# A two-block sandwich kernel: another order of its prologue, and constant matmuls where TensorE would wait in it

## The chip, the cores and the metric

The kernel runs on one core of one Trainium2 chip. The metric is the device time of one execution in microseconds (us), the median of several runs. Engines are named as in the profile: PE is TensorE's matmul, PEld its weight load, DVE is VectorE, ACT is ScalarE, POOL is GpSimd, SP is SyncE, which here only issues DMAs.

## What is computed

Cut to what matters, with x of 16 x 1024 rows of D = 256, E = 8 experts, C = 320 rows each, H = 1024:

```python
def block1(x):                       # x: (16, 1024, 256)
    g = sigmoid(x @ Wg.T + bg)
    h_t = (1 - g_t) * h_(t-1) + g_t * x_t        # along the 1024 rows of a sequence
    return h @ Wo.T + bo

def block2(xf):                      # xf: (16384, 256)
    eid = argmax(softmax(xf @ router_w + router_b))
    rank = number of earlier rows with the same eid
    valid = rank < C
    y_tok = relu(row @ w1[eid] + b1[eid]) @ w2[eid] + b2[eid]     # where valid
    yov = relu(xf @ ow1 + ob1) @ ow2 + ob2                        # elsewhere
    return y_tok where valid, else yov

x = x + layernorm(block1(layernorm(x)))
x = x + layernorm(block2(layernorm(x)))
```

## The kernel before

The 16384 rows are worked in 32 groups of 512 (`GT`), two groups to a sequence, written as pairs (i, v): sequence i, half v. The helper `grp` steps through them. Every fp32 product is made of three matmuls on a high and a low part: `split_product` (L1067 on) multiplies high by high, high by low and low by high; the high part is made by ACT (a copy into the fp32r type), the low part by DVE or POOL (a subtraction). So each operand `X` stands as `X_hi` and `X_lo`.

A group goes through: statistics of its rows (DVE, `stats0`, L712 to L724), 1/sqrt of the variance and the scaled mean (POOL, `deviation`, L372 and L374), the normalised rows `tok` (POOL, `norm0`, L383), their transposes into PSUM tile `psT` (PE, `transposes0`, L1084), `xnT_hi` and `xnT_lo` (L578, L745), the gate product into `psA` (PE, `gate`), the sigmoid `keep` (ACT, L584), the recurrence as a scan (DVE, `recurrence`: `ngx` L755, `hst` L761), `hst_hi` (ACT, L592) and `hst_lo` (POOL, `state_lo`, L424), the product with Wo (PE, `project`), `att` (DVE, `attended`, L767), statistics again (`stats1`), normalisation (ACT, `norm1`, L562), the residual into `x1` (DVE, L780), statistics (`stats2`), `tok2` (POOL, `norm2`, L415), transposes (PE, `transposes1`, L1127), `xfT_hi` and `xfT_lo` (L599, L802), and then the router (`route`), the overflow network on all rows (`layer1`, `layer2`, hidden rows L552, L556, L858) and a scatter of the rows to the experts' buffer `xbuf` in DRAM (POOL). After the 32 groups eight expert steps work on the buffers.

In the loop these are software-pipelined: `step(i, u)` on PE runs the overflow network of group now, `project` of the next and `gate` of the one after it. **The prologue** is what must run before step 0: the whole chain above for group (0,0), up to `xfT_lo`, and the first half, up to the scan, for group (0,1). In it also stand the transposing of Wg and Wo, and the split of the overflow weights ow1 and ow2: four pieces of 128 x 1024, made high by ACT (L662) and low by DVE (L983), out of `stage`, into `W1[1]` and `W2[1]`. Step 0 works a group whose first two tiles cannot overflow (`sure`), so its products have 256 rows and not 512.

Each engine has an order of its own, written by hand in its block function, and semaphores between them; an engine works its instructions strictly in that order. SP's order is x (0,0), Wg, Wo, three bias loads, x (0,1), three broadcasts, router_w, ow1, ow2, b2 and then the clearing of `xbuf` (2.6 MB). ow1 and ow2 share one semaphore, so ACT waits for both.

PSUM tile `psY` (two banks) is written by `layer2` alone and so not used before step 0.

Of the kernel before, what the change touches and what calls it, by code (L numbers as in the profile page):

```python
# [55 lines left out]
def sandwich_kernel(nc, x, Wg, bg, Wo, bo, router_w, router_b, w1, b1, w2, b2, ow1, ob1, ow2, ob2, out):  # L56
# [6 lines left out]
    with ExitStack() as ctx:  # L63
# [474 lines left out]
        def _(act):  # L538
# [118 lines left out]
            xn_hi((0, 1))  # L657
            act.wait_ge(s_w["ow"], 32)
            for m, W in enumerate((W1, W2)):
                for q in range(2):  # L660
                    dst = W[1][0][:].rearrange("p a b -> p (a b)")
                    act.activation(dst[:, q * 1024:(q + 1) * 1024], stage[:, m, q * 1024:(q + 1) * 1024], ACT.Copy)\  # L662
                        .then_inc(s_ow_hi, 1)
# [41 lines left out]
        def _(dve):  # L705
# [271 lines left out]
            def overflow_lo(m):  # L977
                W = (W1, W2)[m]
                for q in range(2):
                    hi = W[1][0][:].rearrange("p a b -> p (a b)")[:, q * 1024:(q + 1) * 1024]  # L980
                    dst = W[1][1][:].rearrange("p a b -> p (a b)")[:, q * 1024:(q + 1) * 1024]
                    dve.wait_ge(s_ow_hi, 2 * m + q + 1)
                    dve.tensor_tensor(dst, stage[:, m, q * 1024:(q + 1) * 1024], hi.bitcast(F32), ALU.subtract)\  # L983
                        .then_inc(s_ow_lo, 1)

            stats0((0, 0))
            for n, W in enumerate((WgT, WoT)):
# [296 lines left out]
```

## Time and profile before

| | before |
|---|---|
| median of 3 runs | 1213.2 us (1212.72 to 1214.56) |
| the profiled execution, its own time | 1212.57 us |
| its span in the trace | 1210.8 us |
| PE busy | 1149.2 us (95%), 7657 matmuls |
| DVE busy | 1015.6 us (84%) |
| ACT busy | 733.8 us (61%) |
| POOL busy | 711.8 us (59%) |
| mean granted TensorE clock | 0.984 |

Times in the trace count from the start of the span. A row of a timeline gives start, duration, engine, line and operation; a count at its end (x4) means that the row merges so many, and its duration is that of them all. Matmuls overlap, so their pace is read from one start to the next. The granted clock is 1.0 at 2.4 GHz and 0.5 at 1.2 GHz.

### The profile page before, as it was taken

To read this page: it belongs to the slowest core of one execution; us is meant where nothing else is said; L and a number is where in the kernel's file an instruction comes from. 1 tells how busy PE (TensorE), PEld (TensorE's weight loads), DVE (VectorE), ACT (ScalarE), POOL (GpSimd) and SP (SyncE) were. 2 spreads that over 40 slices of the span, in tenths; PEclk is the share of its full clock that TensorE was granted. 3 is DMA by queue.
4 is the path that set the end of the run, shared out by engine and by line. 5 is a ranking of instruction groups with operands and counts; after the bars stand their busy time and mean duration, and the time that the engine had idled before them with its cause. 6 is when DMAs were issued, how large, how long until landed. Compare 5 with 4: busy or idle time off the path is not lost.

```text
span 1210.8 us, 24630 instructions
## 1 busy us (share of the span) xinstructions
PE 1149.2 (95%) x7657; PEld 1027.6 (85%) x7657; DVE 1015.6 (84%) x2792; ACT 733.8 (61%) x1293; POOL 711.8 (59%) x826
## 2 busy tenths in 40 slices
PE   5489999999999999999999999999999999899995
PEld 4378888888888888888888888888888888898985
DVE  4688888889888898889888888888889878688883
ACT  3256666666566566666666665556656666678773
POOL 4565666656665656565656666656656664345564
PEclk8799999999999999999999999999999999999997
DMA  8211111111111111111100110011111100445421
GB/s 253 87 36 44 53 50 47 42 37 35 35 35 35 35 35 35 35 35 35 35 28 25 35 35 28 24 35 35 35 35 35 35 18 18 121 136 159 169 81 33
DMA packets 59430, 65.05 MB, mean 54 GB/s; under 512 B 7835, under 2 KB 55629, under 8 KB 59268
## 3 DMA queue, kind: packets, MB, share of 16 engines
q1 hardware_dynamic: 52228, 59.32, 15.3%
q0 software_dynamic: 7168, 5.32, 1.5%
q8 instruction: 16, 0.26, 0.1%
q14 instruction: 18, 0.15, 0.0%
HBM read 40.17 MB, written 38.61 MB: 65 GB/s over the span
## 4 chain that ended last, share of the span: by engine, by line
PE 84%; DVE 6%; POOL 3%; ACT 3%; issue 3%; DMA 0%; DVEq 0%; ACTq 0%; POOLq 0%
PE psY L1171 11%; PE psY L1174 10%; PE psY L1173 10%; PE psH L1071 10%; PE psH L1073 10%; PE psH L1072 10%; PE psA L1071 5%; PE psA L1073 5%; PE psA L1072 5%; PE psT L1127 3%; PE psT L1084 2%; DVE st L712 2%; POOL rstd L372 1%; PE psT L1133 1%; PE psT L1135 1%
## 5 line engine op out<-in xcount | busy, mean ns | idle before, releaser
L372 POOL TENSOR_TENSOR rstd<-veps,mhalf 128x4 f32<-128x4 f32 (+1 forms) x144 | 195.9, 1361 | 386.0 <-DVE nmean L724 386.0
L552 ACT ACTIVATE hid<-psH,biasT 128x512 f32<-128x512 f32 (+2 forms) x320 | 206.7, 646 | 268.8 <-PE psH L1073 264.5
L1171 PE MATMUL psY<-W_hi,hid_hi 128*128 128x256 f32 x1200 | 346.1, 288 | 3.4 <-DVE hid_lo L858 3.4
L1174 PE MATMUL psY<-W_hi,hid_lo 128*128 128x256 f32 x1200 | 339.1, 283 | 0.0
L1173 PE MATMUL psY<-W_lo,hid_hi 128*128 128x256 f32 x1200 | 338.8, 282 | 0.0
L1071 PE MATMUL psH<-xfT_hi,W_hi 128*128 128x512 f32 (+2 forms) x640 | 240.9, 376 | 1.6 <-DVE xfT_lo L802 1.6
L1073 PE MATMUL psH<-xfT_hi,W_lo 128*128 128x512 f32 (+2 forms) x640 | 239.6, 374 | 0.0
L1072 PE MATMUL psH<-xfT_lo,W_hi 128*128 128x512 f32 (+2 forms) x640 | 239.1, 374 | 0.0
L858 DVE TENSOR_TENSOR hid_lo<-hid,hid_hi 128x512 fp32r<-128x512 f32 (+2 forms) x320 | 203.4, 649 | 40.9 <-ACT hid_hi L556 32.1
L1171 PEld LDWEIGHTS psY<-W_hi,hid_hi 128*128 128x128 f32 x1200 | 226.6, 189 | 12.8 <-DVE hid_lo L858 3.1
L1173 PEld LDWEIGHTS psY<-W_lo,hid_hi 128*128 128x128 f32 x1200 | 226.9, 189 | 6.6
L1174 PEld LDWEIGHTS psY<-W_hi,hid_lo 128*128 128x128 f32 x1200 | 226.4, 189 | 0.0
L556 ACT ACTIVATE hid_hi<-hid 128x512 fp32r<-128x512 f32 (+2 forms) x320 | 190.5, 595 | 10.2
L393 POOL DMA_INDIRECT xbuf<-x,idx x128 | 150.4, 1175 | 37.8 <-issue 35.1
L1073 PEld LDWEIGHTS psH<-xfT_hi,W_lo 128*128 128x128 f32 x640 | 120.6, 188 | 21.9
L1071 PEld LDWEIGHTS psH<-xfT_hi,W_hi 128*128 128x128 f32 x640 | 121.0, 189 | 19.5 <-issue 2.4
L1072 PEld LDWEIGHTS psH<-xfT_lo,W_hi 128*128 128x128 f32 x640 | 121.0, 189 | 14.0
L415 POOL TENSOR_SCALAR tok<-x,rstd,nmr 128x256 f32<-128x256 f32 x124 | 109.2, 892 | 8.5 <-POOL nmr L374 8.5
L570 ACT ACTIVATE ysb<-ysb,nmr,rstd 128x256 f32<-128x256 f32 x147 | 76.7, 591 | 45.2 <-POOL nmr L374 44.7
L424 POOL TENSOR_TENSOR hst_lo<-hst,hst_hi 128x512 fp32r<-128x512 f32 x64 | 82.4, 1316 | 10.5 <-ACT hst_hi L592 8.9
L584 ACT ACTIVATE keep<-psA,neg_bg 128x512 f32<-128x512 f32 x64 | 44.0, 689 | 69.0 <-PE psA L1073 69.0
L1071 PE MATMUL psA<-WoT_hi,hst_hi 128*128 128x256 f32 x256 | 75.9, 297 | 2.0 <-POOL hst_lo L424 2.0
(113 smaller groups left out, 2069.2 us busy)
## 6 DMA issues: line engine op xcount, KB each, us to landing
xin<-L_attn_x SPq DMA_DIRECT2D x32, 512.0 KB, 3.5
stage<-L_ffn_w SPq DMA_DIRECT2D x16, 1024.0 KB, 5.6
out<-outt SPq DMA_DIRECT2D x31, 512.0 KB, 2.9
xbuf<-zrow SPq DMA_DIRECT2D x1, 2570.0 KB, 18.7
xin<-xbuf SPq DMA_DIRECT2D x8, 257.0 KB, 5.6
stage<-L_ffn_ow SPq DMA_DIRECT2D x2, 1024.0 KB, 10.1
xbuf<-x,idx POOLq DMA_INDIRECT x128
b_b<-L_ffn_b SPq DMA_DIRECT2D x1, 1024.0 KB, 13.3
```

What stands on the lines that cost most here:

```text
L372: pool.tensor_tensor(rstd[k][:, t0:n], veps[k][:, t0:n], mhalf[:, t0:n], ALU.pow).then_inc(s_rs[k], 1)
L393: pool.indirect_dma_start(out=xbuf, out_offset=bass.IndirectOffsetOnAxis(idx[v][:, t:t + 1], 0), in_=x1[v][:, t, 0:ROW], in_offset=None, b ...
L415: last = pool.tensor_scalar(tok2[:, t, :], x1[v][:, t, 0:D], rstd[2][:, t:t + 1], nmr[2][:, t:t + 1], ALU.mult, ALU.add)
L552: act.activation(hid[j % 2][:, at:n], psH[:, j % 2, at:n], ACT.Relu, bias=bias).then_inc(s_hid, 1)
L556: act.activation(hid_hi[j % 4][:, at:n], hid[j % 2][:, at:n], ACT.Copy).then_inc(s_hid_hi, 1)
L858: dve.tensor_tensor(hid_lo[j % 4][:, at:n], hid[j % 2][:, at:n], hid_hi[j % 4][:, at:n].bitcast(F32), ALU.subtract).then_inc(s_hid_lo, 1)
L1071: pe.matmul(dst, w_hi, r_hi, start=(k == 0), stop=False)
L1072: pe.matmul(dst, w_hi, r_lo, start=False, stop=False)
L1073: return pe.matmul(dst, w_lo, r_hi, start=False, stop=(k == last_k))
L1171: pe.matmul(psY_t[:, t, :], hi, w[0][:, j, :], start=(j == 0 and t % 2 == 0), stop=False, skip_group_check=True)
L1173: pe.matmul(psY_t[:, t, :], hi, w[1][:, j, :], start=False, stop=False, skip_group_check=True)
L1174: last = pe.matmul(psY_t[:, t, :], lo_, w[0][:, j, :], start=False, stop=(j == HC - 1), skip_group_check=True)
```

## The change

It changes nothing in the loop and the experts' part but two waits of step 0. In the prologue:

- SP: ow2 and ow1 are loaded right behind x (0,1), ahead of the broadcasts and router_w, each with a semaphore of its own; SP then waits for both before it issues b2 and the clearing of `xbuf`.
- DVE: makes `tok` of group (0,0), the normalised `att`, `tok2` (by `norm2`, a function that the experts' part already had) and `hst_lo` of both groups, which POOL and ACT made before. The four W_lo pieces stand singly between other work; the statistics of (0,1) come behind `xnT_lo`; the recurrence of (0,1) is cut in two, with `xfT_lo` between the halves.
- ACT: the four W_hi pieces stand singly, the two of ow2 around the first group's sigmoid and `hst_hi`.
- POOL: keeps the four deviations and `tok` of (0,1).
- PE: group (0,0) is transposed a second time into `psA` and not into `psT`, so it need no longer wait for `ngx` of (0,1); that wait and the one for rw_lo stand ahead of `route` in step 0.
- PE: `keep_clock(n)` multiplies `ones` (128 x 128, bf16) by itself, repeated to 512 columns, into `psY`, n times, with nothing that reads it: 5, 3, 5, 12, 3, 24 and 6 times, 58 in all, at the places below.

```diff
             load((0, 1))
+            sp.dma_start(stage_w2(), ow2.rearrange("(c p) d -> p c d", p=P)).then_inc(s_w["ow2"], 16)
+            sp.dma_start(stage_w1(), ow1.rearrange("(c p) h -> p c h", p=P)).then_inc(s_w["ow1"], 16)
...
-            sp.dma_start(stage_w1(), ow1.rearrange("(c p) h -> p c h", p=P)).then_inc(s_w["ow"], 16)
-            sp.dma_start(stage_w2(), ow2.rearrange("(c p) d -> p c d", p=P)).then_inc(s_w["ow"], 16)
+            sp.wait_ge(s_w["ow2"], 16)
+            sp.wait_ge(s_w["ow1"], 16)
...
-            norm0((0, 0))
-            pool.wait_ge(s_tok, 1)
+            deviation(0, (0, 0), TG)
             norm0((0, 1))
-            state_lo((0, 0))
             deviation(1, (0, 0), TG)
-            norm2((0, 0))
-            state_lo((0, 1))
+            deviation(2, (0, 0), TG)
...
             xn_hi((0, 0))
+            overflow_hi(1, 0)
             act.wait_ge(s_biasT, 2)
             sigmoid((0, 0))
-            state_hi((0, 0))
+            state_hi((0, 0), (0,))
+            overflow_hi(1, 1)
+            state_hi((0, 0), (1,))
+            xn_hi((0, 1))
             act.wait_ge(s_w["rw"], 16)
             act.activation(rw[:, :, 0:E], rw_raw[:], ACT.Copy).then_inc(s_rw_hi, 1)
...
-            norm1((0, 0))
+            overflow_hi(0, 0)
+            overflow_hi(0, 1)
             sigmoid((0, 1))
-            xf_hi((0, 0), GT)
+            xf_hi((0, 0), GT, turned=psA)
             state_hi((0, 1))
...
+            def first_rows(k, dst, src):
+                dve.wait_ge(s_nm[k], 1)
+                for t in range(TG):
+                    last = dve.tensor_scalar(dst[:, t, :], src[:, t, 0:D], rstd[k][:, t:t + 1], nmr[k][:, t:t + 1],
+                                             ALU.mult, ALU.add)
+                return last
...
+            stats0((0, 0))
+            turned_lo(0, WgT)
+            first_rows(0, tok, xin[0]).then_inc(s_tok, 1)
+            turned_lo(1, WoT)
             dve.wait_ge(s_biasT, 1)
             dve.tensor_scalar(neg_bg[:], biasT[:, BG:BG + DC], -1.0, None, ALU.mult).then_inc(s_biasT, 1)
+            xn_lo((0, 0))
             stats0((0, 1))
-            xn_lo((0, 0))
+            overflow_lo(1, 0)
             recurrence((0, 0))
-            dve.wait_ge(s_rw_hi, 1)
-            dve.tensor_tensor(rw[:, :, E:2 * E], rw_raw[:], rw[:, :, 0:E].bitcast(F32), ALU.subtract).then_inc(s_rw_lo, 1)
+            state_lo((0, 0))
             xn_lo((0, 1))
+            overflow_lo(1, 1)
             dve.wait_ge(s_w["bcast"], 48)
             attended((0, 0))
             stats1((0, 0))
-            overflow_lo(0)
+            overflow_lo(0, 0)
+            dve.wait_ge(s_att, 2)
+            first_rows(1, att, att).then_inc(s_u, 1)
             residual1((0, 0))
             stats2((0, 0))
-            recurrence((0, 1))
-            overflow_lo(1)
-            xf_lo((0, 0), GT)
+            overflow_lo(0, 1)
+            dve.wait_ge(s_x1, 1)
+            norm2((0, 0), x1, TG)
+            recurrence((0, 1), (0,))
+            xf_lo((0, 0), GT, turned=psA)
+            recurrence((0, 1), (1,))
+            dve.wait_ge(s_rw_hi, 1)
+            dve.tensor_tensor(rw[:, :, E:2 * E], rw_raw[:], rw[:, :, 0:E].bitcast(F32), ALU.subtract).then_inc(s_rw_lo, 1)
+            state_lo((0, 1))
             stats0((1, 0))
...
+            def keep_clock(n):
+                for _ in range(n):
+                    pe.matmul(psY[:, 0, :], ones[:], ones[:].unsqueeze(1).to_broadcast([P, TG, P]), start=True, stop=True)
+
             pe.wait_ge(s_const, 1)
+            keep_clock(5)
...
                     layer1(now, 0, GT, W1[1], at=sure(now) * P)
+                    if not live(grp(i, u, -1), NG):
+                        pe.wait_ge(s_rw_lo, 1)
+                        pe.wait_ge(s_ngx, cnt(nxt, 2, 2))
                     route(now)
...
+            keep_clock(3)
             transposes0((0, 0))
+            keep_clock(5)
             pe.wait_ge(s_wT_lo, 2)
             gate((0, 0))
+            keep_clock(12)
             pe.wait_ge(s_ngx, cnt((0, 0), 2, 2))
             transposes0((0, 1))
+            keep_clock(3)
             project((0, 0))
             gate((0, 1))
-            transposes1((0, 0), TG)
-            pe.wait_ge(s_rw_lo, 1)
+            keep_clock(24)
+            pe.wait_ge(s_tok2, 1)
+            pe.wait_ge(s_keep, cnt((0, 1), 2, 2))
+            for c in range(DC):
+                for t in range(TG):
+                    last = pe.transpose(psA[:, c, t * P:(t + 1) * P], tok2[:, t, c * P:(c + 1) * P], ident[:])
+                last.then_inc(s_T1, 1)
+            keep_clock(6)
             pe.wait_ge(s_ow_lo, 4)
```

On DVE, behind the statistics of `att` of group (0,0), before (`mv`, `veps`, `nmean` are steps of the statistics, `x_0` is `x1`):

```order
L983 TENSOR_TENSOR W_lo<-stage,W_hi 128x1024 [waits s_ow_hi] x2
L780 TENSOR_TENSOR x_0<-att,xin 128x4x256 [waits s_u]
L712 BN_STATS st<-x_0 128x6 [waits s_x1]
L712 BN_STATS st<-x_0 128x6 x3
L719 BN_AGGR mv<-st 128x2 [waits s_st2]
L719 BN_AGGR mv<-st 128x2 x3
L723 TENSOR_SCALAR veps<-mv 128x4 [waits s_ag2,s_nm2]
L724 TENSOR_SCALAR nmean<-mv 128x4
L755 SCALAR_TENSOR_TENSOR ngx<-keep,psT 128x512 [waits s_keep]
```

and in the changed kernel (its `tok` is the tile `tok2`):

```order
L986 TENSOR_TENSOR W_lo<-stage,W_hi 128x1024 [waits s_ow_hi]
L996 TENSOR_SCALAR att<-att,rstd,nmr 128x256 [waits s_nm1,s_att]
L996 TENSOR_SCALAR att<-att,rstd,nmr 128x256 x3
L783 TENSOR_TENSOR x_0<-att,xin 128x4x256 [waits s_u]
L715 BN_STATS st<-x_0 128x6 [waits s_x1]
L715 BN_STATS st<-x_0 128x6 x3
L722 BN_AGGR mv<-st 128x2 [waits s_st2]
L722 BN_AGGR mv<-st 128x2 x3
L726 TENSOR_SCALAR veps<-mv 128x4 [waits s_ag2,s_nm2]
L727 TENSOR_SCALAR nmean<-mv 128x4
L986 TENSOR_TENSOR W_lo<-stage,W_hi 128x1024 [waits s_ow_hi]
L900 TENSOR_SCALAR tok<-x_0,rstd,nmr 128x256 [waits s_T1,s_nm2,s_x1]
```

Both normalisations now stand in DVE's own queue, each behind one W_lo piece, and the scan of (0,1) behind the second of them.

On DVE, the first group's recurrence and what follows it, before:

```order
L755 SCALAR_TENSOR_TENSOR ngx<-keep,psT 128x512 [waits s_keep]
L761 SCALAR_TENSOR_TENSOR hst<-keep,ngx 128x512 [waits s_ngx]
L997 TENSOR_TENSOR rw<-rw_raw,rw 128x2x8 [waits s_rw_hi]
L745 TENSOR_TENSOR xnT_lo<-psT,xnT_hi 128x512 [waits s_xn_hi,s_gate]
L745 TENSOR_TENSOR xnT_lo<-psT,xnT_hi 128x512 [waits s_xn_hi]
L767 TENSOR_TENSOR att<-psA,bo_b 128x512 [waits s_wo,s_w_bcast]
```

and in the changed kernel:

```order
L758 SCALAR_TENSOR_TENSOR ngx<-keep,psT 128x512 [waits s_keep]
L764 SCALAR_TENSOR_TENSOR hst<-keep,ngx 128x512 [waits s_ngx]
L1007 TENSOR_TENSOR hst_lo<-hst,hst_hi 128x512 [waits s_h_hi,s_scan] x2
L748 TENSOR_TENSOR xnT_lo<-psT,xnT_hi 128x512 [waits s_xn_hi,s_gate]
L748 TENSOR_TENSOR xnT_lo<-psT,xnT_hi 128x512 [waits s_xn_hi]
L986 TENSOR_TENSOR W_lo<-stage,W_hi 128x1024 [waits s_ow_hi]
L770 TENSOR_TENSOR att<-psA,bo_b 128x512 [waits s_wo,s_w_bcast]
```

`hst_lo` came to this queue from POOL, and a W_lo piece stands ahead of `att`.

On PE, from the end of the first group's gate to its product with Wo, before (only the first row of each kind of the last product):

```order
L1073 MATMUL psA<-xnT_hi,WgT_lo 128x512
L1084 MATMUL psT<-ident,tok 128x128 [waits s_tok,s_ngx]
L1084 MATMUL psT<-ident,tok 128x128 x7
L1071 MATMUL psA<-WoT_hi,hst_hi 128x256 [waits s_h_lo,s_h_hi,s_keep]
L1072 MATMUL psA<-WoT_lo,hst_hi 128x256
```

and in the changed kernel:

```order
L1110 MATMUL psA<-xnT_hi,WgT_lo 128x512
L1090 MATMUL psY<-ones 128x512 x12
L1121 MATMUL psT<-ident,tok 128x128 [waits s_tok,s_ngx]
L1121 MATMUL psT<-ident,tok 128x128 x7
L1090 MATMUL psY<-ones 128x512 x3
L1108 MATMUL psA<-WoT_hi,hst_hi 128x256 [waits s_h_lo,s_h_hi,s_keep]
L1109 MATMUL psA<-WoT_lo,hst_hi 128x256
```

The constant matmuls have no wait of their own: twelve stand ahead of the transposes of (0,1), three between them and the product.

## Rows read from the trace of the kernel before

**Rows 1.** The page: busy time of PE, and its granted clock in 40 slices

```profile
PE 1149.2 (95%) x7657; PEld 1027.6 (85%) x7657; DVE 1015.6 (84%) x2792; ACT 733.8 (61%) x1293; POOL 711.8 (59%) x826
PEclk8799999999999999999999999999999999999997
```

**Rows 2.** Stretches: length, busy us of PE, PEld, DVE, ACT, POOL; granted clock, DMA, GB/s

```profile
18.30:20.20 1.90, 0.16 (x1) 0.00 (x0) 1.86 (x3) 1.17 (x2) 0.00 (x0) 1.00 1.02 358
23.90:27.20 3.30, 3.29 (x15) 3.30 (x16) 0.49 (x2) 3.08 (x4) 0.00 (x0) 0.50 1.05 251
35.00:47.00 12.00, 0.00 (x0) 0.00 (x0) 9.24 (x17) 2.18 (x5) 7.01 (x6) 0.61 0.16 46
49.06:59.30 10.24, 8.62 (x54) 7.34 (x54) 7.04 (x23) 4.12 (x9) 6.06 (x8) 0.72 0.41 146
50.70:54.60 3.90, 3.82 (x14) 2.80 (x15) 2.54 (x11) 1.49 (x4) 3.49 (x4) 0.50 0.65 218
76.00:80.00 4.00, 4.00 (x19) 3.47 (x18) 3.16 (x11) 1.48 (x4) 3.23 (x4) 0.67 0.28 99
193.00:500.00 307.00, 307.00 (x2026) 272.18 (x2025) 267.83 (x750) 187.43 (x318) 193.25 (x227) 1.00 0.11 34
```

**Rows 3.** Timeline, POOL, in the prologue

```profile
8.23 2.18 POOL L383 TENSOR_SCALAR tok<-xin,rstd,nmr 128x256 f32<-128x256 f32 x4 [0.25 <-POOL nmr L374]
20.50 3.26 POOL L424 TENSOR_TENSOR hst_lo<-hst,hst_hi 128x512 fp32r<-128x512 f32 x2 [5.60 <-ACT hst_hi L592]
31.69 1.91 POOL L372 TENSOR_TENSOR rstd<-veps,mhalf 128x4 f32<-128x4 f32 x1 [7.92 <-DVE nmean L724]
39.67 1.01 POOL L372 TENSOR_TENSOR rstd<-veps,mhalf 128x4 f32<-128x4 f32 x1 [5.75 <-DVE nmean L724]
41.81 5.33 POOL L415 TENSOR_SCALAR tok<-x,rstd,nmr 128x256 f32<-128x256 f32 x4 [0.24 <-POOL nmr L374]
50.47 2.51 POOL L424 TENSOR_TENSOR hst_lo<-hst,hst_hi 128x512 fp32r<-128x512 f32 x2 [3.33 <-ACT hst_hi L592]
```

**Rows 4.** Timeline, DVE and ACT, from the first group's recurrence to step 0

```profile
18.40 1.22 DVE L761 TENSOR_TENSOR_SCAN hst<-keep,ngx 128x512 f32<-128x512 f32 x1
28.60 0.69 DVE L767 TENSOR_TENSOR att<-psA,bo_b 128x512 f32<-128x512 f32 x1 [0.99 <-PE psA L1073]
29.32 1.40 DVE L712 BATCH_NORM_STATS2 st<-att 128x6 f32<-128x256 f32 x4
31.52 2.35 DVE L983 TENSOR_TENSOR W_lo<-stage,W_hi 128x1024 fp32r<-128x1024 f32 x2
33.96 2.07 ACT L562 ACTIVATE att<-att,nmr,rstd 128x256 f32<-128x256 f32 x4 [6.98 <-POOL nmr L374]
36.07 1.23 DVE L780 TENSOR_TENSOR x<-att,xin 128x1024 f32<-128x1024 f32 x1 [2.20 <-ACT att L562]
58.02 1.28 DVE L767 TENSOR_TENSOR att<-psA,bo_b 128x512 f32<-128x512 f32 x2
```

**Rows 5.** Timeline, DVE in the experts' part: four rows normalised by DVE

```profile
1016.68 1.38 DVE L897 TENSOR_SCALAR tok<-x,rstd,nmr 128x256 f32<-128x256 f32 x4 [0.21 <-POOL nmr L374]
```

**Rows 6.** Timeline, PE: transposes and products at either clock

```profile
16.21 0.63 PE L1073 MATMUL psA<-xnT_hi,WgT_lo 128*128 128x512 f32 x1
16.64 0.63 PE L1071 MATMUL psA<-xnT_hi,WgT_hi 128*128 128x512 f32 x1
31.15 0.40 PE L1072 MATMUL psA<-xnT_lo,WgT_hi 128*128 128x512 f32 x1
31.38 0.39 PE L1073 MATMUL psA<-xnT_hi,WgT_lo 128*128 128x512 f32 x1
47.20 1.97 PE L1127 MATMUL psT<-ident,tok 128*128 128x128 f32 x8 [14.72 <-POOL tok L415]
60.41 1.03 PE L1084 MATMUL psT<-ident,tok 128*128 128x128 f32 x8
```

**Rows 7.** DMA issues at 6.72 us: KB each, us from issue to landing

```profile
stage<-L_ffn_ow SPq DMA_DIRECT2D x1, 1024.0 KB, 11.3
```

More of the change, by code:

```diff
@@ L164, in sandwich_kernel @@
         s_xbuf0 = sem("s_xbuf0")
-        s_w = {n: sem(f"s_w_{n}") for n in ("wg", "wo", "rw", "ow", "bias", "bcast", "b2")}
+        s_w = {n: sem(f"s_w_{n}") for n in ("wg", "wo", "rw", "ow1", "ow2", "bias", "bcast", "b2")}
         s_const = sem("s_const")
@@ L585, in sigmoid, with state_hi, xf_hi @@
                         .then_inc(s_keep, 1)
-            def state_hi(g):
+            def state_hi(g, cs=range(DC)):
                 i, v = g
                 act.wait_ge(s_wo, cnt(g, 2, 0))
-                for c in range(DC):
+                for c in cs:
                     act.wait_ge(s_scan, cnt(g, 2, c + 1))
                     act.activation(hst_hi[:, c, :], hst[v][:, c, :], ACT.Copy).then_inc(s_h_hi, 1)
-            def xf_hi(g, n, base=0):
+            def xf_hi(g, n, base=0, turned=psT):
                 act.wait_ge(s_l1, cnt(g, HC, 0) + HC * base)
@@ L598, in xf_hi @@
                     act.wait_ge(s_T1, cnt(g, 2, c + 1) + 2 * base)
-                    act.activation(xfT_hi[:, c, 0:n], psT[:, c, 0:n], ACT.Copy).then_inc(s_xf_hi, 1)
+                    act.activation(xfT_hi[:, c, 0:n], turned[:, c, 0:n], ACT.Copy).then_inc(s_xf_hi, 1)
             def logits_out(g):
@@ L649, in step, with overflow_hi @@
                     state_hi(far)
+            def overflow_hi(m, q):
+                dst = (W1, W2)[m][1][0][:].rearrange("p a b -> p (a b)")
+                act.wait_ge(s_w[("ow1", "ow2")[m]], 16)
+                act.activation(dst[:, q * 1024:(q + 1) * 1024], stage[:, m, q * 1024:(q + 1) * 1024], ACT.Copy)\
+                    .then_inc(s_ow_hi, 1)
             xn_hi((0, 0))
+            overflow_hi(1, 0)
             act.wait_ge(s_biasT, 2)
             sigmoid((0, 0))
-            state_hi((0, 0))
+            state_hi((0, 0), (0,))
+            overflow_hi(1, 1)
+            state_hi((0, 0), (1,))
+            xn_hi((0, 1))
             act.wait_ge(s_w["rw"], 16)
             act.activation(rw[:, :, 0:E], rw_raw[:], ACT.Copy).then_inc(s_rw_hi, 1)
[L657 to L663, printed above, removed]
-            norm1((0, 0))
+            overflow_hi(0, 0)
+            overflow_hi(0, 1)
             sigmoid((0, 1))
-            xf_hi((0, 0), GT)
+            xf_hi((0, 0), GT, turned=psA)
             state_hi((0, 1))
@@ L746, in xn_lo, with recurrence @@
                         .then_inc(s_xn_lo, 1)
-            def recurrence(g):
+            def recurrence(g, cs=range(DC)):
                 i, v = g
@@ L752, in recurrence @@
                     dve.wait_ge(s_h_lo, cnt(grp(i, v, -2), 2, 2))
-                for c in range(DC):
+                for c in cs:
                     dve.wait_ge(s_keep, cnt(g, 2, c + 1))
@@ L797, in stats2, with xf_lo @@
                 moments(2, g, TG)
-            def xf_lo(g, n, base=0):
+            def xf_lo(g, n, base=0, turned=psT):
                 for c in range(DC):
                     dve.wait_ge(s_xf_hi, cnt(g, 2, c + 1) + 2 * base)
-                    dve.tensor_tensor(xfT_lo[:, c, 0:n], psT[:, c, 0:n], xfT_hi[:, c, 0:n].bitcast(F32),
+                    dve.tensor_tensor(xfT_lo[:, c, 0:n], turned[:, c, 0:n], xfT_hi[:, c, 0:n].bitcast(F32),
                                       ALU.subtract).then_inc(s_xf_lo, 1)
@@ L975, in step, with overflow_lo, turned_lo @@
                     stats3(now, TG, t0=sure(now))
-            def overflow_lo(m):
+            def overflow_lo(m, q):
+                cols = slice(q * 1024, (q + 1) * 1024)
                 W = (W1, W2)[m]
[L979 to L987, printed above, removed]
+                hi = W[1][0][:].rearrange("p a b -> p (a b)")[:, cols]
+                dst = W[1][1][:].rearrange("p a b -> p (a b)")[:, cols]
+                dve.wait_ge(s_ow_hi, 2 * (1 - m) + q + 1)
+                dve.tensor_tensor(dst, stage[:, m, cols], hi.bitcast(F32), ALU.subtract).then_inc(s_ow_lo, 1)
+            def turned_lo(n, W):
                 dve.wait_ge(s_wT_hi, n + 1)
```

9 lines of the change are left out of this document (added).

## The prediction

> **What bounds the kernel now.** First the page. PE is busy for 95% of the span, and its slices of the granted clock are full but for the first three and the last [rows 1]. Then the stretches. In the loop PE is busy 307.00 us of 307 at full clock [rows 2], and the change touches nothing there. So what can be won or lost lies before that state is reached. The stretch from 35 to 47 us shows what kind of time this is: PE does nothing at all, while DVE works 9.2 us and POOL 7.0 [rows 2]. Then the timeline, to see which work PE stands for. It is a chain through all engines for group (0,0), and I cut it at four points: the transposes of `tok`, which wait for POOL, 8.23 + 2.18 = 10.4 us; `att` ready at 28.60 + 0.69 = 29.3; `tok2` ready at 41.81 + 5.33 = 47.1; `att` of group (0,1), in step 0, ready at 58.02 + 1.28 = 59.3 [rows 3, 4]. From the last point on, both kernels have the same instructions in the same order.
>
> The clock is the second matter. A 512-column matmul starts 0.43 us after the one before it at 16.2 us, and 0.23 us at 31.2 us [rows 6]: these are the two levels, 1.2 and 2.4 GHz. The granted clock was full at 18.3 to 20.2 us, when PE stood but for 0.16 us, and half at 23.9 to 27.2; half again at 50.7 to 54.6, after the long wait; and 0.67 in 76 to 80 [rows 2]. Eight transposes take 1.97 us at the low level and 1.03 at the high one [rows 6].
>
> **The change, term by term**, against the profiled execution's own 1212.57 us (span 1210.8).
>
> *Term 1, to `att` of (0,0), now 29.3 us.* `tok` by DVE: four of its operations take 1.38 us [rows 5] against POOL's 2.18 [rows 3], with one hop less, so the transposes start at about 9.4 and not 10.5. If the clock is up by then, they give back 0.9 (1.97 to 1.03), and the twelve gate matmuls, which take 4.5 us now, nearly 3.0: the gate ends at about 15.5, otherwise near 18. But then DVE is the queue that counts. Behind `xnT_lo` (about 12.8) stand the statistics of (0,1), 2.3 us (1.40, the aggregation 0.38, two small ones and their gaps, as from 29.32 to the W_lo at 31.52 [rows 4]), one W_lo of 1.2 (half of 2.35 [rows 4]), and two halves of the recurrence at 0.7 + 1.22 each [rows 4]: 12.8 + 2.3 + 1.2 + 3.9 = 20.2. `hst_lo` by DVE is priced by DVE's subtractions, 0.65 each, and ends at 21.5, where POOL ended it at 20.50 + 3.26 = 23.8 [rows 3]. That gain of 2.3 us is not what PE gets, because in its own order the transposes of (0,1) come first, and their `tok` is still POOL's. It now starts only after the statistics at 15.1, so at about 17.3, and meets DVE's two scans (1.22 each) and two `hst_lo` (0.65 each), 3.7 us in all.
>
> What such a meeting costs is in rows 3: `tok2` on POOL took 5.33 us beside DVE's scans and W_lo, where the same four operations took 2.18 us at 8.23; `hst_lo` took 3.26 beside a scan and 2.51 alone. The ends are 19.8 (2.2 us, nothing lost) and 22.6 (5.3 us); I take 22.3, by the nearer row. The Trainium skill, page "SBUF — State Buffer", § Who interferes with whom, says that a DVE instruction with two SBUF inputs and a GpSimd instruction that reads SBUF exclude each other, the loser blocking fully. Full exclusion would put `tok` of (0,1) near 23; without any, it would be ready before `ngx` and term 1 would be 2 us better. The trace agrees in direction: `tok2` lost 5.33 - 2.18 = 3.1 us beside a scan and two W_lo, some 3.6 us of such work [rows 3, 4].
>
> The transposes then end at 23.3 (or 24.3 at half clock). The three constant matmuls behind them are on the path, since `hst_lo` is ready: 0.7 or 1.3 us. A bf16 128 x 512 matmul is not in the trace; bounds are the 128 x 512 rows at either clock, 0.23 and 0.43 [rows 6]. Below that nothing is expected, as the column count is the same. The product of 24 matmuls of 256 columns takes 2.8 us at full and 5.1 at half clock (half the 512-column steps [rows 6]), and DVE's `att` 0.7: 27.6 at full clock, 31.2 at half. The clock may well be half here: PE's twelve constant matmuls end at 18 or so and 4 us of wait follow, longer than the 1.9 us after which it was seen halved [rows 2]. Rising on the way gives about 28.9. **Term 1: -0.4 us, from -2.4 to +1.9.**
>
> *Term 2, from `att` to `tok2`, now 17.8 us.* New: statistics 2.3; deviation on POOL 1.01 for rstd, and 0.3 for nmr with its hops, plus 0.5 because one W_lo lies beside it (1.91 against 1.01 beside two [rows 3]): 1.8; normalise on DVE 1.4 [rows 5]; residual 1.25 [rows 4]; statistics 2.3; deviation 1.8; normalise 1.4. Sum 12.3. What goes is ACT's 2.07 with its hops, most of POOL's 5.33, and the second W_lo of each pair, which moves ahead of term 2 or into a wait. **Term 2: -5.5 us, from -6.2 to -4.3** (the upper end if each deviation stays at 1.91 + 0.5).
>
> PE's 24 constant matmuls lie in this wait: 5.5 us or 10.3 us out of about 10, behind `gate((0, 1))`, which ends near 31 or 32. At full clock they cost nothing; at half they reach 41 or 42, about when `tok2` is ready.
>
> *Term 3, from `tok2` to `att` of (0,1), now 12.2 us.* Here DVE becomes the bound. From the start of `xfT_lo` to the end of `att` it is busy 7.0 of 10.2 us now [rows 2]. The same work stays, and to it come what the old kernel had before `tok2` was ready, two times ngx and scan, 2 x (0.7 + 1.25), what POOL did in 2.51 us [rows 3], `hst_lo`, 2 x 0.65, and rw_lo, some 0.3: 7.0 + 3.9 + 1.3 + 0.3 = 12.5, with 0.5 for the hops inside chains of small operations 13.0, without an idle gap. PE's transposes, six constant matmuls and 12 products of step 0 fit beside it at full clock; at half, 1.97 + 2.6 us stand against 3.5 us of DVE, and add about 1. **Term 3: +0.9 us, from +0.6 to +2.4.**
>
> *Term 4, SP.* ow2 and ow1 move ahead of the broadcasts. ow2 landed 11.3 us after its issue, last of a queue of some 2.8 MB [rows 7]; issued at 4.3, and behind x (0,1) only, it should land near 11.5, before ACT wants it at 12. b2 and the clearing of `xbuf` are held until about 14.5 and end near 30 as now; step 0 wants them after 40. Cost 0. If ow2 came as late as before, 4.3 + 11.3 = 15.6, ACT would reach the sigmoid at 16.6, about 1 us late.
>
> *Term 5, the clock after step 0.* At 76 to 80 us it was 0.67 [rows 2]: some 2.7 us at half level, worth 1.3 us. A shifted kernel may miss that or not: 0, from -1.3 to +1.
>
> Sum: -0.4 - 5.5 + 0.9 = -5.0. I add -0.3 because the clock, half for the first 3.9 us of step 0 now [rows 2], may be up there in some executions. So 1212.57 - 5.3 = 1207.3 for an execution like the profiled one. The median of the runs was 0.6 above that execution, so 1207.9 as a median.
>
> **The rivals.**
>
> *A. The constant matmuls hold the clock throughout.* Then gate, product, transposes and step 0's first 3.9 us all run at 2.4 GHz: term 1 -1.9, term 3 +0.6, 1.5 us more from step 0 and term 5: -8.5, a time of 1204.7. For it: 58 matmuls stand in just those waits. Against it: two of the waits remain 4 us long. Chance 0.22.
>
> *B. DVE and POOL get in each other's way more than my bounds, and DVE's queue, now the longest, passes each delay on.* Three normalisations (4.2 us), two pairs of `hst_lo` (2.6 us) are new to it. If `tok` of (0,1) ends at 24, deviations take 2.4 us each and term 3 is at +2.4, the sum is -2.0: 1211.2. Chance 0.13.
>
> *C. Slower: the constant matmuls don't raise the clock and delay the real ones.* Place: PE's own queue, which has no way past them. At half level they add 0.6 ahead of the first gate, 1.0 ahead of the transposes of (0,1), 1.3 ahead of the product, some 2 ahead of the second transposes (24 x 0.43 behind a gate that itself takes 5 us and ends late), 1.0 ahead of step 0: 5.9, while gate and product at half cost 3.5 more than at the full clock that they had in part. Sum -5.3 + 9 = +3.7: 1216.9. It decides from the point where more than 5.3 us of them lie on the path. Against it: the clock did rise in each stretch in which PE was busy throughout. Chance 0.03.
>
> *D. The prologue's gain is absorbed by something due later.* x (1,0) is loaded after `x1`, which also comes earlier, and the loop is PE-bound, so nothing waits at a fixed time. 1213. Chance 0.04.
>
> **The numbers.** My forecast 0.58, the rivals as given. The range takes in A, and B's better side: 1203.8 to 1211. About 0.2% (2.4 us) is what a measurement of this kernel can tell from no change. Faster by more: forecast, A and most of B, 0.91; within it: the rest of B and D, 0.06; slower 0.03.
>
> **What would show it.** In the profile after: `tok2` ready at about 41 us (term 2) and `att` of (0,1) at about 54; the wait of PE for `tok2` shorter by the constant matmuls; `tok` of (0,1) on POOL at over 4 us; DVE without gaps from `tok2` to step 0; the loop from 200 us on at 307 of 307. I am wrong if `tok` of (0,1) takes 2.2 us, if the first gate starts after 13.9 us, or if the loop's pace itself differs.

## The result, and the profile after

| | before | after |
|---|---|---|
| median of the runs (6 each) | 1213.11 us (1212.29 to 1214.56) | 1208.89 us (1207.86 to 1210.47) |
| ratio, 95% interval | | 0.9964 [0.9953, 0.9976] |
| profiled execution, its own time | 1212.57 us | 1210.47 us |
| its span | 1210.8 us | 1208.7 us |

The changed kernel is faster by 4.2 us as a median. The profiled execution of the changed kernel was the longest of its six, that of before among the shorter ones, so the two traces differ by only 2.1 us, and they can account for only that half of the gain. The executions of the kernel before lie either between 1212.1 and 1213.2 us or between 1213.6 and 1214.9, and how many of each kind a set holds moves its median by up to 1.5 us, so kernels of different sets are compared below by their own medians, with the ratios beside them.

First the page of the changed kernel, busy time and granted clock; it answers to [rows 1]:

```profile
PE 1161.0 (96%) x7715; PEld 1032.3 (85%) x7715; DVE 1007.0 (83%) x2808; ACT 732.8 (61%) x1289; POOL 692.4 (57%) x814
PEclk8899999999999999999999999999999999999998
```

PE has the 58 constant matmuls more (7715 against 7657) and is 11.8 us longer "busy"; that is about what the constant matmuls take, so this number says nothing about the gain. The first slices of the clock hardly changed.

The stretches, with the columns of [rows 2]:

```profile
18.30:20.20 1.90, 0.00 (x0) 0.00 (x0) 1.68 (x3) 1.50 (x2) 1.90 (x2) 1.00 1.01 233
23.90:27.20 3.30, 3.30 (x15) 2.67 (x13) 2.50 (x3) 2.59 (x4) 0.00 (x0) 0.50 1.09 283
41.00:48.00 7.00, 4.49 (x17) 3.04 (x18) 5.63 (x10) 1.71 (x3) 0.90 (x2) 0.52 0.90 297
43.45:56.02 12.57, 12.02 (x74) 9.69 (x75) 11.69 (x30) 5.39 (x11) 3.07 (x6) 0.83 0.39 141
71.50:75.00 3.50, 3.50 (x19) 3.50 (x18) 2.50 (x10) 2.23 (x4) 2.89 (x3) 0.51 0.21 75
193.00:500.00 307.00, 307.00 (x2040) 272.58 (x2038) 265.19 (x752) 188.73 (x321) 189.03 (x226) 1.00 0.10 33
1046.00:1052.00 6.00, 5.03 (x28) 5.03 (x29) 3.37 (x8) 1.06 (x3) 0.83 (x1) 0.72 0.27 84
```

The loop is as it was: 307.00 of 307 at full clock. The clock is half in the first product with Wo, again from 41 to 48 us and from 71.5 to 75, and, what before does not have (1.00 there), it falls in the experts' part.

The timeline of POOL in the prologue, answering to [rows 3]:

```profile
14.59 1.92 POOL L374 TENSOR_TENSOR rstd<-veps,mhalf 128x4 f32<-128x4 f32 x1 [6.47 <-DVE nmean L727]
16.59 0.90 POOL L376 TENSOR_TENSOR nmr<-nmean,rstd 128x4 f32<-128x4 f32 x1
17.74 4.12 POOL L385 TENSOR_SCALAR tok<-xin,rstd,nmr 128x256 f32<-128x256 f32 x4 [0.25 <-POOL nmr L376]
32.44 1.91 POOL L374 TENSOR_TENSOR rstd<-veps,mhalf 128x4 f32<-128x4 f32 x1 [10.58 <-DVE nmean L727]
39.78 1.92 POOL L374 TENSOR_TENSOR rstd<-veps,mhalf 128x4 f32<-128x4 f32 x1 [5.15 <-DVE nmean L727]
```

The timeline of DVE, answering to [rows 4] (DVE's line numbers are 3 higher now):

```profile
14.42 1.22 DVE L986 TENSOR_TENSOR W_lo<-stage,W_hi 128x1024 fp32r<-128x1024 f32 x1
16.27 1.22 DVE L764 TENSOR_TENSOR_SCAN hst<-keep,ngx 128x512 f32<-128x512 f32 x1
18.11 1.26 DVE L764 TENSOR_TENSOR_SCAN hst<-keep,ngx 128x512 f32<-128x512 f32 x1
19.29 0.69 DVE L1007 TENSOR_TENSOR hst_lo<-hst,hst_hi 128x512 fp32r<-128x512 f32 x1
20.20 0.69 DVE L1007 TENSOR_TENSOR hst_lo<-hst,hst_hi 128x512 fp32r<-128x512 f32 x1 [0.22 <-ACT hst_hi L591]
29.02 0.69 DVE L770 TENSOR_TENSOR att<-psA,bo_b 128x512 f32<-128x512 f32 x1 [0.65 <-PE psA L1110]
32.27 1.22 DVE L986 TENSOR_TENSOR W_lo<-stage,W_hi 128x1024 fp32r<-128x1024 f32 x1
34.74 1.38 DVE L996 TENSOR_SCALAR att<-att,rstd,nmr 128x256 f32<-128x256 f32 x4 [1.25 <-POOL nmr L376]
42.07 1.38 DVE L900 TENSOR_SCALAR tok<-x,rstd,nmr 128x256 f32<-128x256 f32 x4 [1.24 <-issue]
54.74 1.28 DVE L770 TENSOR_TENSOR att<-psA,bo_b 128x512 f32<-128x512 f32 x2
```

Three points of the chain can be read off: `att` of (0,0) ready at 29.02 + 0.69 = 29.71 us (29.29 before), `tok2` at 42.07 + 1.38 = 43.45 (47.14), `att` of (0,1) at 54.74 + 1.28 = 56.02 (59.30). So the stretches between are 13.74 and 12.57 us, against 17.85 and 12.16. And the timeline of PE, with the waits:

```profile
12.48 0.47 PE L1108 MATMUL psA<-xnT_hi,WgT_hi 128*128 128x512 f32 x1 [0.72 <-DVE xnT_lo L748]
15.37 2.76 PE L1090 MATMUL psY<-ones 128*128 128x512 bf16 x12
22.00 1.94 PE L1121 MATMUL psT<-ident,tok 128*128 128x128 f32 x8 [3.87 <-POOL tok L385]
23.74 1.49 PE L1090 MATMUL psY<-ones 128*128 128x512 bf16 x3
24.66 0.78 PE L1108 MATMUL psA<-WoT_hi,hst_hi 128*128 128x256 f32 x1
32.75 5.35 PE L1090 MATMUL psY<-ones 128*128 128x512 bf16 x24
43.51 1.97 PE L1276 MATMUL psA<-ident,tok 128*128 128x128 f32 x8 [5.41 <-DVE tok L900]
45.27 2.65 PE L1090 MATMUL psY<-ones 128*128 128x512 bf16 x6
1046.97 0.87 PE L1164 MATMUL psT<-ident,tok 128*128 128x128 f32 x6 [2.19 <-DVE tok L900]
```

Twelve constant matmuls take 2.76 us and leave 3.87 of wait; 24 take 5.35 and leave 5.41. Behind both waits the eight transposes take 1.94 and 1.97 us, the duration at half clock [rows 6]. Behind the last row the products of the experts' part are paced at 0.21 us where 0.12 is their full pace: the transposes stood 2.95 us earlier than before (1049.92), the end of the span only 2.1.

### The profile page after: what moved, and what is told of

Its sections match the earlier page's. It is cut to its first block, busy times and chain, and to the rows that moved or that the text cites. A ratio compares the mean times of both kernels' runs of the same rounds, so it can differ in the third digit from the quotient of the medians.

```text
span 1208.7 us, 24748 instructions
## 1 busy us (share of the span) xinstructions
PE 1161.0 (96%) x7715; PEld 1032.3 (85%) x7715; DVE 1007.0 (83%) x2808; ACT 732.8 (61%) x1289; POOL 692.4 (57%) x814
## 4 chain that ended last, share of the span: by engine, by line
PE 83%; DVE 6%; issue 3%; POOL 3%; ACT 3%; DMA 1%; DVEq 0%; ACTq 0%; POOLq 0%; SPq 0%
PE psY L1208 11%; PE psY L1211 10%; PE psY L1210 10%; PE psH L1108 9%; PE psH L1110 9%; PE psH L1109 9%; PE psA L1108 5%; PE psA L1110 5%; PE psA L1109 5%; PE psT L1164 3%; PE psT L1121 2%; DVE st L715 2%; POOL rstd L374 2%; PE psT L1170 1%; PE psT L1172 1%
## 5 line engine op out<-in xcount | busy, mean ns | idle before, releaser
L395 POOL DMA_INDIRECT xbuf<-x,idx x128 | 145.0, 1133 | 37.8 <-issue 34.8
L1110 PEld LDWEIGHTS psH<-xfT_hi,W_lo 128*128 128x128 f32 x640 | 120.3, 188 | 21.9
L1109 PEld LDWEIGHTS psH<-xfT_lo,W_hi 128*128 128x128 f32 x640 | 120.6, 188 | 13.9
L417 POOL TENSOR_SCALAR tok<-x,rstd,nmr 128x256 f32<-128x256 f32 x120 | 93.1, 788 | 7.9 <-POOL nmr L376 7.9
L426 POOL TENSOR_TENSOR hst_lo<-hst,hst_hi 128x512 fp32r<-128x512 f32 x60 | 76.3, 1295 | 4.8 <-ACT hst_hi L591 4.5
```

Source lines behind the costliest of these rows:

```text
L395: pool.indirect_dma_start(out=xbuf, out_offset=bass.IndirectOffsetOnAxis(idx[v][:, t:t + 1], 0), in_=x1[v][:, t, 0:ROW], in_offset=None, b ...
L417: last = pool.tensor_scalar(tok2[:, t, :], x1[v][:, t, 0:D], rstd[2][:, t:t + 1], nmr[2][:, t:t + 1], ALU.mult, ALU.add)
L1109: pe.matmul(dst, w_hi, r_lo, start=False, stop=False)
L1110: return pe.matmul(dst, w_lo, r_hi, start=False, stop=(k == last_k))
```

## The experiments

All kernels were timed in five rounds against the kernel before. Its median was 1212.87 us in the first set of kernels, 1214.39 in the second, 1214.23 in the third. "Chain" is my theory: the rearranged chain brings the gain and the constant matmuls little. "Clock" is its rival: they bring it.

**First set: parts of the change.** The changed kernel again.

> The changed kernel once more, as the anchor for the other three. Its profiled execution lost 1.2 us to a drop of the clock at 1048 us. If that drop belongs to that execution alone, this trace is 3.2 us or more ahead of the kernel before at the end; if it belongs to the kernel, a clock drop near 1048 us shows here too. Ratio to the kernel before about 0.9965.

Measured 1208.44 us (1207.66 to 1209.57), ratio 0.9958 [0.9944, 0.9971]. In its trace `att` of (0,1) is 4.06 us earlier than before, and the fall in the experts' part is there again; it costs 1.3 us. So it was no accident of one execution; in how many of the others it stands is not known.

The constant matmuls taken out:

```diff
-                for _ in range(n):
+                for _ in range(0):
```

> The changed kernel without any of its 58 constant matmuls. Theory 'chain' (the gain is the shorter chain through DVE; the constant matmuls are worth little): within 0.8 us of the changed kernel, either side, and tok2 ready at 42 to 44.5 us. Rival 'clock' (the constant matmuls carry the gain by raising the clock early): 2 us or more slower than the changed kernel, the first gate at half clock and so ended near 17.5 us in place of 15.4.

Measured 1207.93 us (1207.28 to 1208.21), 0.9955 [0.9941, 0.9968]. The same as with them, as "chain" had it. Its timelines of POOL and PE:

```profile
17.57 5.06 POOL L385 TENSOR_SCALAR tok<-xin,rstd,nmr 128x256 f32<-128x256 f32 x4 [0.25 <-POOL nmr L376]
9.55 1.97 PE L1121 MATMUL psT<-ident,tok 128*128 128x128 f32 x8 [2.16 <-DVE tok L996]
22.78 1.94 PE L1121 MATMUL psT<-ident,tok 128*128 128x128 f32 x8 [5.17 <-POOL tok L385]
24.37 0.56 PE L1108 MATMUL psA<-WoT_hi,hst_hi 128*128 128x256 f32 x1
```

The first transposes are now at half clock, and the first gate starts 0.5 us later (13.02). But in both kernels `tok` of (0,1) is late, PE waits, and the product that follows is at half clock. What the constant matmuls ahead of the gate give, they lose again: the transposes of (0,1) start at 22.00 us with them and at 22.78 without, but from there to the product it takes 2.66 us with the three in between and 1.59 without, so the product starts at 24.66 and at 24.37.

The old prologue with the same 58 constant matmuls:

```diff
+            keep_clock(3)
             transposes0((0, 0))
+            keep_clock(5)
             pe.wait_ge(s_wT_lo, 2)
             gate((0, 0))
+            keep_clock(12)
             pe.wait_ge(s_ngx, cnt((0, 0), 2, 2))
             transposes0((0, 1))
+            keep_clock(3)
             project((0, 0))
             gate((0, 1))
+            keep_clock(24)
             transposes1((0, 0), TG)
+            keep_clock(6)
```

> The old prologue with the same counts of constant matmuls at the same places. 'Chain': no gain, between 0 and 2 us slower than the kernel before, since the twelve ahead of the second transposes (5 us at half clock) stand where PE waits only 1.8 us. 'Clock': 2 us or more faster than the kernel before.

Measured 1208.63 us (1207.33 to 1208.9), 0.996 [0.9946, 0.9973]. My expectation fell: in the old order the constant matmuls alone bring as much as the whole change. Its PE timeline, with POOL's `tok` of (0,1):

```profile
12.63 2.16 POOL L383 TENSOR_SCALAR tok<-xin,rstd,nmr 128x256 f32<-128x256 f32 x4 [0.24 <-POOL nmr L374]
16.19 2.76 PE L1058 MATMUL psY<-ones 128*128 128x512 bf16 x12
18.79 1.04 PE L1089 MATMUL psT<-ident,tok 128*128 128x128 f32 x8
43.54 1.97 PE L1132 MATMUL psT<-ident,tok 128*128 128x128 f32 x8 [9.36 <-POOL tok L415]
```

Here `tok` of (0,1) is ready at 14.8 us, before the gate ends. The twelve fill the wait for `ngx` to the end, the transposes (1.04 us) and the product run at full clock, and `att` of (0,0) is ready at 25.81, 3.48 us earlier than before. Of these, 1.89 us are there when the product starts (22.02 against 23.91): they come from the gate at full clock, behind the first thirteen constant matmuls. The other 1.59 are the product at full clock, behind the twelve and the three. From `att` to `tok2` it takes 17.68 us as ever. The changed order took this cover away: it put `tok` of (0,1) behind later statistics and beside DVE's scans, so that the same twelve ended 3.9 us too soon.

More constant matmuls in the changed kernel, 28 for 12 and 44 for 24:

> The changed kernel with 28 and 44 constant matmuls in the two long waits in place of 12 and 24, 6.5 and 10.2 us at full clock, which fills the waits of 6.6 and 10.8 us. If the clock then stays at full from 10 us on: second transposes 0.9 us shorter, product 1.1 us shorter, transposes of tok2 0.9 us shorter, together about 2 us better than the changed kernel, as DVE covers the last. If the clock drops all the same they run at half and hold up the real work: 2 to 6 us slower.

Measured 1206.24 us (1206.03 to 1206.59), 0.9943 [0.9929, 0.9956], 2.2 us under the changed kernel of its set. Its PE timeline:

```profile
15.32 6.22 PE L1090 MATMUL psY<-ones 128*128 128x512 bf16 x28
21.94 1.06 PE L1121 MATMUL psT<-ident,tok 128*128 128x128 f32 x8 [0.41 <-POOL tok L385]
30.24 9.67 PE L1090 MATMUL psY<-ones 128*128 128x512 bf16 x44
41.00 1.09 PE L1276 MATMUL psA<-ident,tok 128*128 128x128 f32 x8 [1.09 <-DVE tok L900]
```

Both sets of transposes are at full clock with waits of 0.41 and 1.09 us left. `att` of (0,0) is ready at 27.21, `tok2` at 40.94, `att` of (0,1) at 53.58, 1.7 to 2.5 earlier than in the two traces with 12 and 24. The 2.2 us are what was expected.

**Second set: what keeps DVE and POOL apart.** `tok` of (0,1) by DVE, between the halves of the recurrence:

```diff
-            norm0((0, 1))
+            deviation(0, (0, 1), TG)
...
-            recurrence((0, 0))
+            recurrence((0, 0), (0,))
+            dve.wait_ge(s_T0, 2)
+            first_rows(0, tok, xin[1], 2).then_inc(s_tok, 1)
+            recurrence((0, 0), (1,))
```

> The changed kernel, but tok of group (0,1) is made by DVE, between the two halves of the first recurrence, and not by POOL. Theory 'POOL beside DVE' (that tok, 4.1 to 5.1 us with DVE's scans and hst_lo beside it and with nmr late, is what holds the second transposes at 22 us whatever the clock does, and the wait ahead of them is what lets the clock fall): the transposes start at 20 us or before, at full clock, att of (0,0) is ready 2 us or more earlier than in the changed kernel, total 2 to 3.5 us faster than it. Rival 'DVE is the bound there': the added 1.4 us in DVE's queue gives it all back, total within 0.7 us.

Measured 1207.46 us (1205.86 to 1207.52), 0.9943 [0.9929, 0.9956]. On DVE it takes 1.38 us, and PE's wait shrinks from 3.87 to 1.26 us:

```profile
18.03 1.38 DVE L996 TENSOR_SCALAR tok<-xin,rstd,nmr 128x256 f32<-128x256 f32 x4
20.06 1.09 PE L1124 MATMUL psT<-ident,tok 128*128 128x128 f32 x8 [1.26 <-DVE ngx L758]
```

`att` of (0,0) is ready at 26.71, over 2 us ahead of the two traces of the changed kernel, as expected, and `att` of (0,1) at 52.53, 6.8 us earlier than before, but the experts' part loses 1.3 of it. Against the changed kernel's medians (1208.44 and 1208.89) it is 1.0 to 1.4 us faster, where 2 to 3.5 were expected.

The W_lo pieces away from the two deviations (`overflow_lo(0, 0)` and `(0, 1)` to either side of `xn_lo((0, 1))`, the W_hi of ow1 on ACT ahead of `xn_hi((0, 1))`):

> The changed kernel, but no W_lo piece lies beside the deviations of att and x1: they move to the two waits around xnT_lo of (0,1), and the W_hi pieces of ow1 ahead of xnT_hi. 'POOL beside DVE': rstd takes 1.0 us in place of 1.9 in both, from nmean to the normalised rows 1.5 in place of 2.4, total 1 to 1.8 us faster than the changed kernel, less up to 1 us if W_lo now stretches tok of (0,1). Rival (rstd's 1.9 us has another cause): rstd stays at 1.9 us.

Measured 1208.79 us (1207.74 to 1209.35), 0.9954 [0.9941, 0.9968]: nothing gained. POOL's timeline shows both sides of it:

```profile
17.69 6.21 POOL L385 TENSOR_SCALAR tok<-xin,rstd,nmr 128x256 f32<-128x256 f32 x4 [0.25 <-POOL nmr L376]
34.34 1.01 POOL L374 TENSOR_TENSOR rstd<-veps,mhalf 128x4 f32<-128x4 f32 x1 [10.43 <-DVE nmean L727]
40.77 1.01 POOL L374 TENSOR_TENSOR rstd<-veps,mhalf 128x4 f32<-128x4 f32 x1 [5.15 <-DVE nmean L727]
```

Each `rstd` falls from 1.91 to 1.01 us. But the two W_lo now lie beside `tok` of (0,1), which grows from 4.12 to 6.21 us, and `att` of (0,0) comes 2.2 us later than before (1.8 later than in the changed kernel). The expected gain of 1 to 1.8 us, less up to 1, did not come, because both deviations together saved 1.8 us and `tok` cost 2.1.

Both edits together:

> Both of the last two edits. If the two are separate terms they add: 3 to 5 us faster than the changed kernel, so 1204 to 1206 us.

Measured 1206.91 us (1206.04 to 1207.23), 0.9939 [0.9926, 0.9953]. `att` of (0,0) at 28.05, `tok2` at 39.65 (11.6 us between), `att` of (0,1) at 52.01: 7.3 us earlier than before, of which the experts' part loses 1.45. It is 1.5 to 2.0 us faster than the changed kernel, where 3 to 5 were expected: `tok` is free of the two W_lo now, but they stand ahead of `att` of (0,0) in DVE's queue, and this `att` is ready 1.3 us later than in the kernel with only `tok` moved.

Both, with 18, 5 and 36 constant matmuls for 12, 3 and 24:

> Both edits, with 18, 5 and 36 constant matmuls in place of 12, 3 and 24, which fill the waits there at full clock. If the clock's two falls in the prologue are still to be had (1.1 us at the product, 0.9 at each transposes), this is 1 to 2 us faster than with both edits alone; if DVE covers them by then, the same within 0.5 us.

Measured 1205.92 us (1205.76 to 1207.88), 0.9937 [0.9924, 0.9951], 1.0 us lower than the last as a median, but by the ratios hardly (0.9937 against 0.9939), and two of its five executions took 1207.4 and 1207.9 us: not settled. In its trace the 36 end 0.8 us after `tok2` is ready.

**Third set: the waits behind the prologue.** Every fall in the experts' part stood behind one wait of PE, for `tok` of the first expert. Eight constant matmuls there, in the changed kernel:

```diff
+                    for _ in range(8):
+                        pe.matmul(psA[:, 0, :], ones[:], ones[:].unsqueeze(1).to_broadcast([P, TG, P]), start=True, stop=True)
                     transposes1((0, 0), ET, NG)
```

> The changed kernel and eight more constant matmuls (into psA, which nothing uses there) ahead of the transposes for the first expert, where PE waited 2.2 us for tok by DVE and the granted clock then fell for 3.4 us in the profiled executions of the changed kernel. 'PE's wait lets the clock fall': the eight take 8 x 0.23 = 1.8 us out of that wait, the clock stays full there, and the end keeps the loop's offset: 1.2 us less than the changed kernel, 1207.3. 'The fall there has another cause' (it was seen in some kernels with that wait and not in others): it stays, or the eight make no difference: 1208.5.

Measured 1208.11 us (1207.81 to 1209.0), 0.9954 [0.994, 0.9967]. The timeline of PE there:

```profile
1044.79 1.90 PE L1255 MATMUL psA<-ones 128*128 128x512 bf16 x8
1046.68 0.88 PE L1164 MATMUL psT<-ident,tok 128*128 128x128 f32 x6
```

The clock stayed full behind it, and the 3.2 us of lead at these transposes became 3.5 at the end. But this execution had half clock for longer behind step 0 and lost 1.0 us between there and the experts, and its own time was 1209.0, the longest of its five. The median, 1208.11, lies between the two expectations (1207.3 and 1208.5), so the time decides nothing; the trace does for its place. Of the ten traces of kernels without these eight, five have the fall; of the four with them, this one and the next three, none.

Ten more ahead of the second transposes of step 0:

```diff
+                    if run and ahead and not live(grp(i, u, -1), NG):
+                        pe.wait_ge(s_keep, cnt(far, 2, 2))
+                        for _ in range(10):
+                            pe.matmul(psA[:, 0, :], ones[:], ones[:].unsqueeze(1).to_broadcast([P, TG, P]), start=True, stop=True)
                     transposes1(nxt, TG)
```

> The same, and ten more ahead of the second transposes of step 0, where PE waits 2.9 us for tok2 of (0,1) by POOL, behind a wait for keep of the group after, which the transposes imply anyway. The half clock that follows there (some 3.4 us at 71.9 us in the changed kernel) should go: 'PE's wait lets the clock fall': 1.2 + up to 1.5 less than the changed kernel, 1206 to 1207.3. 'Another cause': 1208.5. If the ten delay the transposes, since keep comes late, the wait row for tok2 turns short and the offset worsens by up to 1 us.

Measured 1207.69 us (1207.41 to 1209.09), 0.9953 [0.9939, 0.9966]. The timeline of PE in step 0, and three stretches:

```profile
67.12 2.33 PE L1254 MATMUL psA<-ones 128*128 128x512 bf16 x10
70.23 1.09 PE L1164 MATMUL psT<-ident,tok 128*128 128x128 f32 x8 [0.78 <-POOL tok L417]
46.00:60.00 14.00, 12.93 (x106) 11.79 (x105) 12.92 (x48) 6.70 (x15) 4.76 (x8) 1.00 0.09 29
60.00:90.00 30.00, 27.32 (x176) 22.45 (x175) 25.83 (x74) 17.71 (x34) 18.46 (x23) 1.00 0.14 45
1030.00:1060.00 30.00, 28.67 (x200) 26.02 (x199) 19.56 (x52) 19.17 (x38) 8.29 (x10) 1.00 0.41 117
```

In stretches of 25 us from 50 to 1175 us its clock is 1.00 in every one, where the changed kernel's has 0.93 from 50 to 75, 0.96 from 1025 to 1050 and 0.98 behind that. The profiled execution gains 4.9 us of span on before, where the changed kernel's two gained 2.1 and 3.0. As medians it is 1.2 us under the 1208.89 and 0.75 under the 1208.44 of the changed kernel; the ranges overlap, and 1206 to 1207.3 was expected, so this is the right direction and the size is not settled.

Both places in the kernel with both edits, and in the one with 28 and 44:

> Both places, in the kernel that has tok of (0,1) on DVE and W_lo away from the deviations (1206.9, whose profiled execution had the fall at 1043.6 us and half clock at 68 us). 'PE's wait lets the clock fall': 1.5 + 1.2 less, 1204.2 to 1205. 'Another cause': 1206.9.

> Both places, in the kernel with 28 and 44 constant matmuls (1206.2; no fall in the experts' part in its profiled execution, clock full from 6.2 to 47.2 us). 'PE's wait lets the clock fall': only what step 0 still loses, 0 to 1.2 us: 1205 to 1206.2. 'Another cause': 1206.2. Compared with the kernel before it, it shows whether the two ways of gaining add up.

Measured 1205.85 us (1205.68 to 1206.73), 0.9936 [0.9923, 0.995], and 1206.14 us (1205.9 to 1206.28), 0.9936 [0.9923, 0.995]. The second is where the kernel with 28 and 44 stood without the two places (1206.24), whose profiled execution had no fall at either of them. Its one fall behind the gate was elsewhere: half clock from about 47 to 50 us, behind waits of PE of 1.09, 0.98 and 0.90 us within six. With the two places the same waits (1.10, 0.98 and 0.90) brought none, but the first transposes, behind a wait of 1.93, were at half clock (1.69 us). The first has the lowest median of the study, though by only 0.07 us, and is 2.6 and 3.0 us under the two medians of the changed kernel. Against the same kernel without the places it is 1.1 us better as a median, where I had expected 1.9 or more, and by the ratios (0.9936 against 0.9939, intervals that overlap) hardly at all: what the two places are worth there is not settled.

## Why the prediction was right, and where its terms were off

The time, 1208.9 us, is 1.0 above the 1207.9 forecast and inside the range. Of 5.3 us foreseen, 4.2 came as a median. The terms were stated for the profiled execution, and there less came: they add up to 2.15 us in its trace (2.1 in the spans), and to 3.0 in the second trace of the same kernel. Where the shorter executions gain the rest, no trace shows; that the median lies so near the forecast is in part luck.

**Term 1** (-0.4): +0.4 in the profiled execution, -0.35 in the second one. `tok` of (0,1) ended at 21.9, near the 22.3 taken, but by errors that cancel. Its statistics ended at 14.5 and not 15.1 and `tok` itself took 4.12 us and not 5.0, while its deviation, priced at 2.2 us, took 3.2: the W_lo beside it stretched `rstd` to 1.92 us, and the first scan stretched `nmr` to 0.90, which the sum had not counted. The gate was at full clock. The 3.87 us of wait then halved the clock for transposes and product (0.50 at 23.9 to 27.2 us), the case the text named. Right.

**Term 2** (-5.5, its range ending at -4.3): -4.1. This is the term that was mis-sized. "Plus 0.5 because one W_lo lies beside it" made 1.8 us of each deviation. One W_lo costs `rstd` as much as two: 1.92 and 1.91 us against 1.01. With `nmr` and the hops that is 2.4 us from `nmean` to the normalisation, twice, 1.2 us above the 1.8 each; the rest is 0.3 in the statistics. The rows fit a simple reason: W_lo runs from 32.27 to 33.49, `rstd` ends at 34.35, 0.86 after it, as if POOL had stood until DVE's instruction was over; a second W_lo would have nothing left to block. The kernel with W_lo moved away confirmed that W_lo is the cause (1.01 both times); that POOL stood for all of it is read from the ends of the rows.

**Term 3** (+0.9): +0.4, and DVE was busy 11.69 of 12.57 us, the bound as foreseen. **Term 4** (0): ACT waited 1.16 us for `stage` and began its W_hi at 12.60; the sigmoid behind it, at 14.24, waited for PE's gate all the same, so it cost nothing. **Term 5** (0): +0.3 between step 0 and the loop's end. What I had not in the list is a fall of the clock 1000 us later, behind the wait of PE that is 1.70 us before and 2.19 now: 0.85 us in the profiled execution, 1.3 in the second.

PE's wait for `tok2` fell from 14.72 to 5.41 us, by more than its 24 constant matmuls. Of the other signs named, three held (`tok` of (0,1) over 4 us, DVE almost without gaps, the first gate before 13.9, at 12.48) and the loop is unchanged; `tok2` came at 43.45 and not 41, `att` of (0,1) at 56.0 and not 54.

**Rival A** (the clock held throughout) was not this kernel, but its place was right: with 28 and 44 it gained 2.2 us more. **Rival B** was half right, as its deviations of 2.4 us came, without the rest. **C** didn't come: all constant matmuls but the three ahead of the product lay in waits, or beside DVE's longer work. **D** didn't: of the 3.28 us of lead of `att` of (0,1), 2.95 were still there at 1047 us.

What the prediction did not see is that the two halves of the change do not add up. By stretches (to `att` of (0,0), to `tok2`, to `att` of (0,1)): before 29.3, 17.9, 12.2; constant matmuls alone 25.8, 17.7, 11.1; rearrangement alone 29.2, 13.7, 12.6; the change 29.7, 13.7, 12.6. Alone they gained 4.2 and 4.9 us by medians, together 4.4. The rearrangement won the second stretch. It spoiled the first, in which the constant matmuls alone were worth 3.5 us, and it made DVE the bound of the third, in which they alone were worth 1.1.

Left open: why in some executions PE's wait before the first expert brings the fall and in others not (it came behind waits of 1.83, 1.98, 2.02, 2.09 and 2.19 us, and not behind 1.70, three times, 1.75 and 1.84), and why the kernels with `tok` of (0,1) on DVE have 2.1 us between span and own time where the others have 1.8. The rearrangement was run only as a whole, so that its gain in the second stretch comes from the normalisations on DVE is read from the rows and not shown by a run for each move.

## What to carry over

Constant matmuls paid here only where they came near the end of the wait (in the old order to the end; with 28 and 44 to 0.41 and 1.09 us of it): size each set by the wait row that is left behind it, and size it again whenever the producer moves. Before work is moved from POOL to DVE, list which DVE instructions with two SBUF inputs will lie beside the POOL ones on the path, for a POOL instruction of 1.01 us took 1.9 here beside such a one. And after a gain early in a kernel, look at the granted clock to the very end, since it can be given back at a wait a thousand microseconds later.
